# One core, attention and mixture of experts: output products by halves, GpSimd's weight chunks in another order, expert transposes three tiles ahead, last result rows ahead of the last down products

## What is computed

```python
Q, K = relu(x @ Wq.T + bq) * decay, relu(x @ Wk.T + bk) * decay    # per head, decay = exp(-pos / n)
V = x @ Wv.T + bv
out = (Q @ (K.T @ V)) / (Q @ K.sum(over tokens) + 1e-6)
x = layernorm(x + out @ Wo.T + bo)
w, ids = top2(softmax(x @ w_gate)); w = w / w.sum()
routed = sum over the token's 2 experts of w * (silu(x @ gate_e) * (x @ up_e)) @ down_e
shared = (silu(x @ sh_gate) * (x @ sh_up)) @ sh_down
x = layernorm(x + routed + shared)
```

## Time and profile before

| | |
|---|---|
| median of 3 runs | 256.34 us (256.05 to 257.27) |
| profiled execution | 257.67 us, its span 255.7 us |
| PE, busy | 231.2 us, 90% |
| weight loads (PEld), busy | 197.1 us, 77% |
| DVE, busy | 152.4 us, 60% |
| ACT, busy | 115.9 us, 45% |
| POOL, busy | 137.3 us, 54% |
| mean granted clock of PE | 0.972 of full speed |
| DMA | 31.72 MB, 124 GB/s mean |

### The profile page before, as it was taken

The page is one execution under the profiler, slowest core; times in us unless marked ns, Lnnn a source line. Parts: engine busy times, 40 slices in busy tenths (PEclk is TensorE's granted clock), DMA queues, the critical chain, the costliest instruction groups (busy, mean ns, idle before and its releaser), DMA issues.

```text
span 255.7 us, 5039 instructions
## 1 busy us (share of the span) xinstructions
PE 231.2 (90%) x1440; PEld 197.1 (77%) x1440; DVE 152.4 (60%) x526; ACT 115.9 (45%) x298; POOL 137.3 (54%) x161
## 2 busy tenths in 40 slices
PE   8989989989989999999993999999999989994960
PEld 2458888788879788789991988888888878893960
DVE  2783363276546959669645466666666624999521
ACT  2262613832570731752603466666666644324600
POOL 0072486899688888656582066555555560030420
PEclk9999999999999999999998699999999999998896
DMA  5943038321441121222532255455555305952222
GB/s 167 368 161 103 3 101 311 86 66 39 110 137 62 44 84 41 85 83 103 174 135 70 82 146 157 140 151 160 154 167 144 118 19 155 342 163 82 75 91 82
DMA packets 21579, 31.72 MB, mean 124 GB/s; under 512 B 3248, under 2 KB 14257, under 8 KB 21556
## 3 DMA queue, kind: packets, MB, share of 16 engines
q1 hardware_dynamic: 17552, 22.46, 29.3%
q0 software_dynamic: 3456, 8.43, 9.5%
q10 hardware_dynamic: 548, 0.53, 0.6%
HBM read 19.70 MB, written 12.76 MB: 127 GB/s over the span
## 4 chain that ended last, share of the span: by engine, by line
PE 62%; DVE 18%; DMA 6%; issue 5%; POOL 3%; ACT 3%; SPq 1%; POOLq 0%; DVEq 0%; ACTq 0%
PE bank L329 17%; PE bank L331 13%; PE bank L330 13%; PE bank L598 4%; POOL x_slots L1325 3%; DVE x L1209 3%; PE bank L371 3%; DMA x_slots<-x,slot 3%; DMA k_sb<-in_batt 2%; PE bank L435 2%; PE bank L619 2%; PE bank L475 2%; PE bank L385 2%; DVE xt_raw L1021 2%; DVE wa_lo L904 2%
## 5 line engine op out<-in xcount | busy, mean ns | idle before, releaser
L1369 POOL DMA_INDIRECT y_pairs<-x_t,dst x40 | 38.9, 973 | 36.5 <-DVE dst L1167 30.1
L329 PE MATMUL bank<-wf_hi,ot_hi 128*128 x120 | 42.2, 352 | 1.5 <-issue 1.0
L1325 POOL DMA_INDIRECT x_slots<-x,slot x32 | 31.9, 998 | 14.7 <-issue 8.3
L330 PE MATMUL bank<-wf_lo,ot_hi 128*128 x120 | 34.7, 289 | 0.0
L331 PE MATMUL bank<-wf_hi,ot_lo 128*128 x120 | 34.6, 289 | 0.0
L329 PEld LDWEIGHTS bank<-wf_hi,ot_hi 128*128 128x128 f32 x120 | 23.5, 196 | 8.2 <-issue 7.2
L329 PE MATMUL bank<-x1t_hi,wf_hi 128*128 128x512 f32 x64 | 26.0, 406 | 0.5 <-DVE xt_raw L1021 0.5
L331 PE MATMUL bank<-x1t_hi,wf_lo 128*128 128x512 f32 x64 | 25.3, 395 | 0.0
L330 PE MATMUL bank<-x1t_lo,wf_hi 128*128 128x512 f32 x64 | 25.2, 394 | 0.0
L1306 POOL TENSOR_TENSOR wf_lo<-stage,wf_hi 128x512 fp32r<-128x512 f32 x18 | 23.1, 1286 | 1.5
L330 PEld LDWEIGHTS bank<-wf_lo,ot_hi 128*128 128x128 f32 x120 | 23.7, 197 | 0.0
(11 more groups left out here) (175 smaller groups left out, 622.9 us busy)
## 6 DMA issues: line engine op xcount, KB each, us to landing
o_sb<-x_slots SPq DMA_DIRECT2D x40, 129.0 KB, 2.1
stage<-in_wffn SPq DMA_DIRECT2D x18, 256.0 KB, 2.7
x<-in_x SPq DMA_DIRECT2D x4, 512.0 KB, 6.6
out<-x SPq DMA_DIRECT2D x8, 256.0 KB, 2.1
xt_raw<-in_xT SPq DMA_DIRECT2D x3, 512.0 KB, 6.1
x_slots<-fill SPq DMA_DIRECT2D x9, 129.0 KB, 2.8
x<-in_watt SPq DMA_DIRECT2D x4, 256.0 KB, 6.1
k_sb<-y_pairs SPq DMA_DIRECT2D x2, 512.0 KB, 4.4
```

What stands on the lines that cost most here:

```text
L329: mm(o, w_hi, m_hi, start=start, stop=False, **more)
L330: mm(o, w_hi, m_lo, start=False, stop=False, **more)
L1325: pool.indirect_dma_start(out=x_scat, out_offset=bass.IndirectOffsetOnAxis(ap=slot[:, j, t:t + 1], axis=0), in_=x1[:, t, :], in_offset=Non ...
L1369: pool.indirect_dma_start(out=y_scat, out_offset=bass.IndirectOffsetOnAxis(ap=dst[:, j:j + 1], axis=0), in_=ey[:, u, :], in_offset=None, b ...
```

## The change

- `o_transposed` transposes half 0 of all four tiles, then half 1, and signals each half. `proj_o` issues the bias products of tiles 0 and 1 at once, waits for half 0, makes its products for tiles 0 and 1, then the same for half 1; tiles 2 and 3 follow one after the other as before.
- PE's wait for `bf_ready` goes from ahead of the first `k_t_v` into the first `ranks`.
- GpSimd's list is written out: chunks 0 to 3 before the low part of input 2, 4 to 6, norm 0, 7 to 10, the low part of input 3, 11 and 12, rows and norm 1, 13 to 17; only then the first scatter. A wait for the landing of batch 0's scatter is added ahead of batch 1's.
- Expert tiles: transposes of tile s+3 in step s, in four banks (4, 7, 3, 6) and four buffers for the rounded parts. The second transpose has one bank (2) and waits for the low part of the tile before; the down product has one bank (5) and waits for the copy of the tile before. The rounded activations lie in `b_row`, which is free by then.
- Batch 3's `last_rows` for all four tiles come ahead of its first down product, in a bank for each tile (4, 7, 0, 1). Each tile's end is signalled by itself; VectorE takes moments of tiles 0 and 1, then of 2, applies the norm to 0 and 1, takes the moments of 3, applies 2 and 3; GpSimd makes the scales for 0 and 1, for 2, and for 3.

```diff
-        xe_hi, xe_lo = (o[:, 0, :].rearrange("p (a k n) -> p a k n", a=2, k=KD) for o in (ot_hi, ot_lo))
-        he_hi, he_lo = (o[:, 1, 0:2 * IM].rearrange("p (a n) -> p a n", a=2) for o in (ot_hi, ot_lo))
+        xe_hi, xe_lo = (o[:, :, :].rearrange("p k (a n) -> p (k a) n", a=TB // 2).rearrange(
+            "p a (k n) -> p a k n", k=KD) for o in (ot_hi, ot_lo))
+        he_hi, he_lo = (b_row[:, n * 2 * IM:(n + 1) * 2 * IM].rearrange("p (a n) -> p a n", a=2) for n in range(2))
+
+        def xe_bank(u):
+            return bank[(4, 7, 3, 6)[u]][:, 0:KD * P]
+
...
         lg_bank = bank[7][:, 0:TB * NE]
-
-        def sum_bank(b, h):
-            return bank[(4, 7)[h]] if b == NB - 1 else bank[5 + h]
+        h_bank, y_bank = bank[2], bank[5]
+
+        def last_sum(t):
+            return bank[(4, 7, 0, 1)[t]][:, 0:D]
...
-                for t in range(TB):
-                    pe.wait_ge(S["o_out"], TB * b + t + 1)
-                    for m in range(KD):
+                for m in range(KD):
+                    for t in range(TB):
+                        if m == 0:
+                            pe.wait_ge(S["o_out"], TB * b + t + 1)
                         last = nc.tensor.transpose(bank[(4, 7)[m]][:, t * P:(t + 1) * P],
                                                    o_sb[:, t, m * P:(m + 1) * P], ident)
-                last.then_inc(S["ot_mm"], 1)
+                    last.then_inc(S["ot_mm"], 1)
 
             def proj_o(b):
-                pe.wait_ge(S["ot_hi_out"], KD * (b + 1))
-                pe.wait_ge(S["ot_lo_out"], KD * (b + 1))
+                def home(t):
+                    return bank[5 + t % 2][:, 0:D]
+
+                def bias(t):
+                    mm(home(t), one_f[:, :], b_row[:, 2 * D:3 * D], start=True, stop=False)
+
+                def product(t, k):
+                    c = slice(t * P, (t + 1) * P)
+                    w = slice(WO + k * D, WO + (k + 1) * D)
+                    return split3(home(t), ot_hi[:, k, c], ot_lo[:, k, c], wa_hi[:, w], wa_lo[:, w], False, k == KD - 1)
+
+                bias(0)
+                bias(1)
                 if b == 0:
                     pe.wait_ge(S["ow_split"], 2)
-                for t in range(TB):
-                    if t >= 2:
-                        pe.wait_ge(S["r_out"], TB * b + t - 1)
-                    o = bank[5 + t % 2][:, 0:D]
-                    mm(o, one_f[:, :], b_row[:, 2 * D:3 * D], start=True, stop=False)
-                    for k in range(KD):
-                        c = slice(t * P, (t + 1) * P)
-                        w = slice(WO + k * D, WO + (k + 1) * D)
-                        last = split3(o, ot_hi[:, k, c], ot_lo[:, k, c], wa_hi[:, w], wa_lo[:, w], False, k == KD - 1)
-                    last.then_inc(S["y_mm"], 1)
+                for k in range(KD):
+                    pe.wait_ge(S["ot_hi_out"], KD * b + k + 1)
+                    pe.wait_ge(S["ot_lo_out"], KD * b + k + 1)
+                    for t in (0, 1):
+                        last = product(t, k)
+                        if k == KD - 1:
+                            last.then_inc(S["y_mm"], 1)
+                for t in (2, 3):
+                    pe.wait_ge(S["r_out"], TB * b + t - 1)
+                    bias(t)
+                    product(t, 0)
+                    product(t, 1).then_inc(S["y_mm"], 1)
 
             def x1_transposed(b):
                 pe.wait_ge(S["x1_out"], TB * (b + 1))
...
 
                 pe.wait_ge(S["hot_out"], b + 1)
+                if b == 0:
+                    pe.wait_ge(S["bf_ready"], 1)
                 if b >= 2:
...
 
-                pe.wait_ge(S["shh_out"], CS * (b + 1))
-                pe.wait_ge(S["shl_out"], CS * (b + 1))
+                if h == 0:
...
                     pe.wait_ge(S["sres_out"], 2 * (b - 1) + h + 1)
                 m_hi, m_lo = hh(b)
                 for t in (2 * h, 2 * h + 1):
-                    o = sum_bank(b, h)[:, (t % 2) * D:(t % 2 + 1) * D]
-                    if b == NB - 1:
-                        last_rows(o, t)
+                    o = last_sum(t) if b == NB - 1 else bank[5 + h][:, (t % 2) * D:(t % 2 + 1) * D]
                     for c in range(CS):
                         w = slice(SH_DN + c * D, SH_DN + (c + 1) * D)
                         n = slice(t * P, (t + 1) * P)
                         last = split3(o, m_hi[:, c, n], m_lo[:, c, n], wf_hi[:, w], wf_lo[:, w],
                                       c == 0 and b < NB - 1, c == CS - 1)
-                last.then_inc(S["sdn_mm"], 1)
+                    if b == NB - 1 or t % 2:
+                        last.then_inc(S["sdn_mm"], 1)
 
 
             def first_kv():
...
             proj_q(0)
-            pe.wait_ge(S["bf_ready"], 1)
             pe.wait_ge(S["cst_in"], 16)
             pe.wait_ge(S["small_in"], 32)
...
                 pe.wait_ge(S["eh_out"], j + 1)
-                nc.tensor.transpose(bank[2 + u % 2][:, 0:P], eh[:, u % 2, :], ident).then_inc(S["eht_mm"], 1)
+                if j >= 1:
+                    pe.wait_ge(S["he_lo_out"], j)
+                nc.tensor.transpose(h_bank[:, 0:P], eh[:, u % 2, :], ident).then_inc(S["eht_mm"], 1)
 
             def e_down(j, u, e):
                 pe.wait_ge(S["he_lo_out"], j + 1)
-                split3(bank[5 + u % 2][:, 0:D], he_hi[:, u % 2, :], he_lo[:, u % 2, :],
+                if j >= 1:
+                    pe.wait_ge(S["ey_out"], j)
+                split3(y_bank[:, 0:D], he_hi[:, u % 2, :], he_lo[:, u % 2, :],
                        ex_hi[:, bass.ds(e, 1), KD * 2 * IM:], ex_lo[:, bass.ds(e, 1), KD * 2 * IM:],
                        True, True).then_inc(S["ey_mm"], 1)
 
@@ -630,14 +658,15 @@
             e_transposed(0, 0, 1)
             e_transposed(1, 1, 1)
             pe.wait_ge(S["sh_out"], EARLY_B * CS + AHEAD)
+            e_transposed(2, 2, 1)
             e_gate_up(0, 0, expert0)
-            e_transposed(2, 2, 1)
+            pe.wait_ge(S["sres_out"], EARLY_B * 2)
+            e_transposed(3, 3, 1)
             e_gate_up(1, 1, expert1)
             e_h_transposed(0, 0)
-            e_transposed(3, 3, 1)
+            e_transposed(4, 0, 2)
             e_gate_up(2, 2, expert2)
             e_h_transposed(1, 1)
-            pe.wait_ge(S["sres_out"], EARLY_B * 2)
             e_down(0, 0, expert0)
 
 
...
-                    e_transposed(s + 2, v, i + 2)
+                    if s + 3 < NT:
+                        e_transposed(s + 3, (v + 1) % RING, i + 2 + (v + 1) // RING)
                     e_gate_up(s + 1, (v + 3) % RING, experts[v + 2])
                     e_h_transposed(s, (v + 2) % RING)
...
             shared_gu(3, CS - 1)
             shared_dn(2, 1)
+            for t in range(TB):
+                last_rows(t)
             shared_dn(3, 0)
             shared_dn(3, 1)
 
...
             def ot_hi_out(b):
-                act.wait_ge(S["ot_mm"], b + 1)
                 if b >= 1:
                     act.wait_ge(S["y_mm"], TB * b)
                 for m in range(KD):
+                    act.wait_ge(S["ot_mm"], KD * b + m + 1)
                     copy(ot_hi[:, m, :], bank[(4, 7)[m]][:, :]).then_inc(S["ot_hi_out"], 1)
 
             def x1_apply(b):
...
                     act.wait_ge(ey_st[u], 16 * rounds)
-                copy(ey[:, u, :], bank[5 + u % 2][:, 0:D]).then_inc(S["ey_out"], 1)
+                copy(ey[:, u, :], y_bank[:, 0:D]).then_inc(S["ey_out"], 1)
 
             act.wait_ge(S["y_mm"], T)
             act.wait_ge(S["lg_mm"], NB)
             act.wait_ge(S["num_mm"], T)
             e_x_hi(0, 0)
             e_x_hi(1, 1)
+            e_x_hi(2, 2)
             e_silu(0, 0)
-            e_x_hi(2, 2)
+            e_x_hi(3, 3)
             e_silu(1, 1)
             e_h_hi(0, 0)
-            e_x_hi(3, 3)
+            e_x_hi(4, 0)
...
             act.wait_ge(S["x1lo_out"], KD * NB)
             e_y(0, 0, None)
             for s in range(2, 2 + RING - 1):
...
             e_x_lo(0, 0)
             e_x_lo(1, 1)
+            e_x_lo(2, 2)
             e_h(0, 0)
-            e_x_lo(2, 2)
+            e_x_lo(3, 3)
             e_h(1, 1)
             e_h_lo(0, 0)
-            e_x_lo(3, 3)
+            e_x_lo(4, 0)
             e_h(2, 2)
             e_h_lo(1, 1)
-            with dve.Fori(0, NT // RING - 1) as i:
+            with dve.Fori(0, NT // RING - 2) as i:
                 for w in range(RING):
                     s = i * RING + (w + 2)
-                    e_x_lo(s + 2, w)
+                    e_x_lo(s + 3, (w + 1) % RING)
                     e_h(s + 1, (w + 3) % RING)
                     e_h_lo(s, (w + 2) % RING)
-            e_h(NT - 1, (NT - 1) % RING)
-            for s in (NT - 2, NT - 1):
+            for s in range(NT - RING - 2, NT):
+                if s + 3 < NT:
+                    e_x_lo(s + 3, (s + 3) % RING)
+                if s + 1 < NT:
+                    e_h(s + 1, (s + 1) % RING)
                 e_h_lo(s, s % RING)
...
             def apply_norm(b, t):
```

(53 more changed lines are left out.)

38 lines of the change are left out of this document (20 added, 18 removed).

## The result

Measured beside each other on one chip, the changed kernel takes 249.24 us median (248.68 to 251.06) and the kernel before 256.19 (255.49 to 257.27): ratio 0.974, 95% interval 0.968 to 0.980. The prediction was 243.5 us, range 239.5 to 249.0; 7.0 us were gained instead of 12.8. The profiled execution took 249.33 us (before: 257.67), its span is 247.5 us (before: 255.7).

What follows compares the result with a forecast made beforehand. It took the expert loop as bound by a circle of waits between engines, not by PE; -3.1 to tile 5, -4.8 loop and -4.9 end made -12.8 from 257.67, 244.9, as median 243.5 us, range 239.5 to 249.0.

Steps and rivals of the forecast that it cites:

- Front: Ahead of the experts: moved wait and output products by halves bring PE through the shared products 2.0 us earlier (-1.0 to -3.7).
- row 2's wait: In the output products, row 2 waits for VectorE to read row 0's bank: 0.4 us, four times.
- GpSimd's order: Reordered weight chunks and scatters: POOL's last scatter ends 3.5 us earlier, VectorE's diagonals come next, first gate-up at 138.15 us.
- I expect the low clock again for some 7 us: At the start of the experts: PE idles as long as before, so the clock drops again as long.
- the sum: From the start to expert tile 5: -3.1 us, bounds -1.0 and -5.5.
- 34 x (1.64 - 1.50) = -4.8: Expert loop: 34 tiles fall from 1.64 to 1.50 us each, -4.8 us in all, bounds 0 and -8.2.
- rival 1: Expert loop: PE's address arithmetic is itself the bound, the loop gives nothing, the rest stays: 248.3 us, chance 0.16.
- The circle: Expert loop: gate-up to transposes two tiles further, then to their gate-up, bounds two old tiles at 3.4 us.
- So I cost it at nothing: Expert loop: a single output bank's round trip takes 1.4 us, just under the 1.50 us tile, so adds 0.
- Loads hide: Expert loop: buffers are reused after 6.0 us and loads land in 2.1 us, leaving some 2 us for SyncE's queue.
- The end: Last rows ahead of batch 3's down products: PE's products gain 5.9 us, the whole end 4.9 (bounds -3.4 and -5.9).
- the median of the runs is 1.33 us lower: Whole kernel: step from the profiled 257.67 us to the median 256.34, turning the forecast 244.9 into 243.5.

Runs made afterwards that it cites:

- fixed experts: Changed kernel with each tile's expert fixed at build, no word load or address work on TensorE: 260.64 us, 0.998 of the kernel before; with plain stores 251.77 us, 0.954.
- two banks: Changed kernel with two banks each for transposes, hidden rows and down products, without TensorE's two new waits: 262.56 us, ratio 0.999; with plain stores 253.65 us, 0.961.

## Why the prediction was right or wrong

- Front, -2.0 on PE's side: right in its sum, in part by luck. The last shared product before the experts ends at 132.89 us, before 134.86. The term of row 2's wait was 0.4 us a batch (the 0.35 us in it stand in no row) and measured 0.23; the longer wait ahead of the first ranks, 1.21 us for 0.34, had not been seen, and the two roughly cancel.
- GpSimd's order: POOL's last scatter of rows ends at 128.9 us, 4.6 us earlier (3.5 predicted), and VectorE's eight diagonals are next in line, as said: gate-up 0 starts at 138.04, predicted 138.15.
- The clock: "I expect the low clock again for some 7 us" was wrong, the stretch is 3.4 us. PE idles 0.61, 0.68, 0.70 and 1.87 us in pieces instead of 3.51 at once. At tile 5 the sum is -3.3 instead of -3.1; why the shorter stretch shows no more there was not followed.
- Loop: the step that failed is the term 34 x (1.64 - 1.50) = -4.8; 0.8 came. Most of the miss is its second number. "Nearest is the 1.49 us tile ... with the waits I take 1.50": over the 34 tiles the new order took 53.91/34 = 1.59. The tile of 1.49 us was one without a word to load. The word is loaded once in four tiles (at 151.93 and 158.55 us in the old trace), and the word and the addresses lengthen the new order's groups by 0.66 us over four times 1.40; fixed experts take all of it away. In the old order the word's load ends at 152.5 us, and the transposes behind it start at 152.60 without a gap; in the new one it stands behind the wait for the hidden activations' low part, ends at 155.92, and the transposes wait for it. The added waits, called unpriced, have some 0.3 us of the 0.66 in the shortest groups. It is rival 1 in a form that I had not worked out. That its time, 248.3 us, is 0.9 from the result is in part luck, since the loop gave something and the drain took it back.
- The first number of that term was wrong too: the old order took 54.73/34 = 1.61 us a tile, not 1.64, which is 1.0 us of the miss. A count of weight loads in 50 us (61) is too coarse for it: the faster loop counts 60. The circle itself was read rightly in kind and too long: two neighbouring tiles never take less than 3.18 us in three traces of the old order (3.4 predicted), and 2.88 are seen in the new one.
- "So I cost it at nothing": the single banks' round trip doesn't bind in the steady loop, which was right, but it does where the loop drains and no other tile covers it (0.6 us), and through its waits' instructions. What two banks recover of the whole time stays open, as said above.
- Loads hide: right on the first chip.
- The end, -4.9: right, -5.15, and the bounds held, but two misses cancel. PE's last product comes 8.8 us earlier, 5.3 of them since the shared gate-up (5.9 predicted; from set to set the last rows take 1.30 us, not 1.11), and the chain behind it takes 3.4 us instead of 3.2, where 4.2 had been predicted. Clock and gaps as predicted; the last store took 0.5 us more.
- The range of 239.5 to 249.0 missed by 0.2 us. The loop alone did not do that: "the median of the runs is 1.33 us lower" came from a profiled execution of the kernel before that was longer than its timed ones, while that of the changed kernel is 0.09 us above its median. Of the 5.7 us missing, 4.6 are in the profile (the loop 4.0, the drain 0.6, the last store 0.5, less 0.5 of front and end), and the rest is this step.
- Outside all rivals: on the two other chips where both orders have a trace, the new loop is slower than the old by 7.3 us (64.9 against 57.6) and by some 3.4 (62.7 against 59.2, the latter in the longest of its four executions). The mechanism does not appear in the trace of before; nothing in it could have priced this.
